# Second graph layer's low weight parts on VectorE instead of GpSimd, one behind each head's front part

## What is computed

```python
def gat_layer(x, W, att_src, att_dst, bias, src, dst, heads, out_ch, concat):
    h = (x @ W.T).reshape(n, heads, out_ch)
    a_src = jnp.einsum('nhc,hc->nh', h, att_src)
    a_dst = jnp.einsum('nhc,hc->nh', h, att_dst)
    e = jax.nn.leaky_relu(a_src[src] + a_dst[dst], NEG_SLOPE)
    m = jax.ops.segment_max(e, dst, num_segments=n)
    ex = jnp.exp(e - m[dst])
    denom = jax.ops.segment_sum(ex, dst, num_segments=n)
    alpha = ex / (denom[dst] + EPS)
    out = jax.ops.segment_sum(alpha[:, :, None] * h[src], dst, num_segments=n)
    ...
h = gat_layer(x, W1, att_src1, att_dst1, b1, src, dst, heads=8, out_ch=128, concat=True)
h = jax.nn.relu(h)
out = gat_layer(h, W2, att_src2, att_dst2, b2, src, dst, heads=1, out_ch=768, concat=True)
```

## Time and profile before

| | us |
|---|---|
| median of 3 runs | 1350.22 |
| lowest and highest of them | 1344.23, 1350.96 |
| the profiled execution's own time | 1348.07 |
| its span, first to last instruction | 1346.5 |

### The profile page before, as it was taken

One profiled execution on the slowest core, in us unless ns is written; L12 is line 12 of the kernel. 1 busy time (PEld: TensorE's weight loads), 2 busy tenths in 40 slices (PEclk: granted clock), 3 DMA queues, 4 the chain that ended last, 5 costly groups with the idle time before them and its releaser, 6 DMA issues. The chain is left out here.

```text
span 1346.5 us, 19432 instructions
## 1 busy us (share of the span) xinstructions
PE 1280.1 (95%) x7053; PEld 1099.5 (82%) x7054; DVE 911.3 (68%) x1828; ACT 582.8 (43%) x1013; POOL 127.0 (9%) x123
## 2 busy tenths in 40 slices
PE   5999999999999999999999999999999898899997
PEld 2577659969969997666999999999998778796864
DVE  4477683473473465555859999999998778836623
ACT  2011051351350343334418888888986227502110
POOL 0000010000000000003320000000002018600101
PEclk9999999999999999999999999999999998999899
DMA  9321091410410620003158999999998310007134
GB/s 340 136 94 63 9 359 55 153 71 1 153 71 1 235 95 0 1 24 141 67 209 295 356 382 389 390 386 392 389 382 281 137 28 1 1 1 293 47 105 164
DMA packets 80687, 225.46 MB, mean 167 GB/s; under 512 B 5168, under 2 KB 17008, under 8 KB 80496
## 3 DMA queue, kind: packets, MB, share of 16 engines
q1 hardware_dynamic: 72720, 187.64, 37.7%
q0 software_dynamic: 7904, 36.97, 7.6%
HBM read 197.85 MB, written 26.74 MB: 167 GB/s over the span
## 5 line engine op out<-in xcount | busy, mean ns | idle before, releaser
L2116 DVE TENSOR_TENSOR part_slot<-slot,item_hi 128x768 fp32r<-128x768 f32 x150 | 133.5, 958 | 0.2
L1557 ACT ACTIVATE item_hi<-slot 128x768 fp32r<-128x768 f32 x156 | 118.0, 833 | 23.9 <-DMA slot<-in_e0w 19.6
L2125 DVE TENSOR_TENSOR part_slot<-slot,item_hi 128x768 fp32r<-128x768 f32 x132 | 116.6, 954 | 1.7 <-ACT item_hi L1565 1.3
L1565 ACT ACTIVATE item_hi<-slot 128x768 fp32r<-128x768 f32 x132 | 99.1, 831 | 14.6 <-DMA slot<-in_e0w 14.6
L722 PE MATMUL dve_ps<-item_hi,x_hi 128*128 128x384 f32 x288 | 99.3, 345 | 0.5 <-DVE x_lo L2305 0.3
L722 PE MATMUL act_ps<-item_hi,hid_hi 128*128 128x384 f32 x288 | 98.4, 342 | 0.3 <-DVE hid_lo L2317 0.3
L724 PE MATMUL dve_ps<-item_hi,x_lo 128*128 128x384 f32 x288 | 97.2, 338 | 0.0
L723 PE MATMUL act_ps<-part_slot,hid_hi 128*128 128x384 f32 x288 | 96.8, 336 | 0.0
L724 PE MATMUL act_ps<-item_hi,hid_lo 128*128 128x384 f32 x288 | 96.1, 334 | 0.0
L723 PE MATMUL dve_ps<-part_slot,x_hi 128*128 128x384 f32 x288 | 95.6, 332 | 0.0
L1448 ACT ACTIVATE h_t<-act_ps,par 128x256 f32<-128x256 f32 x36 | 21.1, 585 | 121.5 <-PE act_ps L833 121.5
(11 more groups left out here) (407 smaller groups left out, 3268.9 us busy)
## 6 DMA issues: line engine op xcount, KB each, us to landing
slot<-in_e0w SPq DMA_DIRECT2D x48, 2304.0 KB, 10.4
slot<-in_w SPq DMA_DIRECT2D x9, 2304.0 KB, 9.4
experts<-in_e1w SPq DMA_DIRECT2D x8, 1152.0 KB, 15.3
ea_raw<-in_edge SPq DMA_DIRECT2D x8, 1024.0 KB, 5.5
slot<-in_wqkv SPq DMA_DIRECT2D x3, 2304.0 KB, 14.8
xs<-zrow POOLq DMA_DIRECT2D x2, 3072.0 KB, 15.7
item_x<-xs SPq DMA_DIRECT2D x16, 384.0 KB, 9.6
ys<-item_y POOLq DMA_DIRECT2D x16, 384.0 KB, 6.7
```

Of the source, the lines that this page charges most:

```text
L1557: go(item_hi[j][k][:, :], slot[s][:, k * D:(k + 1) * D], ACT.Copy).then_inc(up_high[j], 1)
L1565: go(item_hi[j][k][:, :], slot[s][:, k * D:(k + 1) * D], ACT.Copy).then_inc(down_high[j], 1)
L2116: vv.tensor_tensor(part_slot[s][:, ks], slot[s][:, ks], item_hi[j][k][:, :].bitcast(F32), ALU.subtract).then_inc(up_low[j], 1)
L2125: vv.tensor_tensor(part_slot[s][:, ks], slot[s][:, ks], item_hi[j][k][:, :].bitcast(F32), ALU.subtract).then_inc(down_low[j], 1)
```

## The change

The eight low parts leave GpSimd's stream. VectorE forms them instead, low part hd behind `graph_front(hd + 2)` in turn hd of its loop (in turns 6 and 7, which have no front left to make, behind `graph_out`). The arithmetic, the wait for the high part and the semaphore that is raised are the same.

```diff
+            def low_second_layer(k):
+                ks = slice(k % 4 * D, (k % 4 + 1) * D)
+                dve.wait_ge(w_high, 2 * DC * L + 3 * DC + k + 1)
+                vv.tensor_tensor(part_slot[2 + k // 4][:, ks], slot[2 + k // 4][:, ks], part_slot[k // 4][:, ks].bitcast(F32), ALU.subtract
+                                 ).then_inc(w_low, 1)
+
...
                 if hd + 2 < GH:
                     graph_front(hd + 2, row_unit(hd + 2), v0)
+                low_second_layer(hd)
             graph_out(GH - 1)
...
-            def low_of(s, block, high, done):
-                pool.wait_ge(w_high, 2 * DC * L + 3 * DC + done + 1)
-                nc.gpsimd.tensor_tensor(part_slot[s][:, block], slot[s][:, block], high.bitcast(F32), ALU.subtract).then_inc(w_low, 1)
-
...
-                for k in {2: (0,), 3: (1,), 4: (2,), 5: (3,), 6: (4,), 7: (5, 6, 7)}.get(g, ()):
-                    ks = slice(k % 4 * D, (k % 4 + 1) * D)
-                    low_of(2 + k // 4, ks, part_slot[k // 4][:, ks], k)
```

## The result

The changed kernel took 1351.38 us, median of 20 runs (1346.67 to 1357.03), against 1347.40 for the kernel before, also 20 runs (1343.21 to 1350.96). The ratio on record is 1.0041 with a 95% interval of 1.0030 to 1.0052: 0.41% slower, or 5.5 us (4.0 to 7.0). It is estimated from all the runs and is not the quotient of the medians: these lie only 3.98 us apart, and the means 5.09 us. The forecast was a loss of 5.75 us.

A forecast was written before the change was run, and what follows sets the result against it. The prediction took VectorE to bound the middle heads of the first graph layer. Five low parts at 0.87 + 0.28 us gave 5.75 us, added to 1348.07 (profile) or 1350.22 (median); middle 1355.0 us, range 1350.3 to 1360.5.

The forecast's parts named there:

- VectorE sets the pace in the middle heads: First graph layer, middle heads: VectorE busy 7.33 of 7.51 us, so work added to its stream adds to the time.
- Five on the path, three hidden: Low parts 1 to 5 delay the weights of heads 2 to 6, 4.35 us; 0, 6 and 7 fall into waits.
- 0.87 us for the operation, 0.28 for the meeting: Each low part on the path costs 0.87 us itself plus 0.28 waiting for GpSimd's second sum, 5.75 us for five.
- The prediction's bound of 0.41: Middle heads: a low part's full wait for GpSimd's second sum, 0.41 us each, would make the loss 6.4 us.
- Nobody waits for the later exponentials: Middle heads: GpSimd's third sum starts some 0.9 us late, making the last exponential later, at no cost.
- The lost race: Rival, middle heads: GpSimd's next sum goes before the waiting low part, 1.24 us more each, 11.9 in all; chance 0.08.
- The clock: Rival: longer TensorE idle time halves its clock before head 7, loss 7.5 to 8.8 us in all; chance 0.38.
- The lower of its two prices: Clock fall before head 7: 3.3 us at half clock costs 1.7 us; the higher price was 3.0.
- The time: Whole kernel: 1355.0 us, the middle of 1353.8 and 1356.0, from a loss of 5.75 us.

The follow-up runs named there:

- e1_covered: Kernel before, with low parts 0, 6 and 7 moved to VectorE and 1 to 5 left on GpSimd; 1344.87 us, ratio 0.9989 to the kernel before.
- e2_path: Kernel before, with low parts 1 to 5 moved to VectorE and 0, 6 and 7 left on GpSimd; 1349.84 us, ratio 1.0031 to the kernel before.
- e13_after_best: Changed kernel, idle time before head 1 filled in place of its `spend`, filling behind heads 1 to 5, `xres` additions behind `out_lo`; 1347.39 us, 1.0018 to kernel before.
- e3_ahead: Changed kernel, with each low part placed ahead of the front on VectorE instead of behind it; 1351.55 us, ratio 1.0039 to the kernel before.
- e4_twice: Changed kernel, with each of low parts 1 to 5 formed twice in a row on VectorE; 1363.94 us, ratio 1.0121 to the kernel before.
- e9_after_start: Changed kernel, with 32 unused matmul calls behind head 0's turns and without head 1's `spend`; 1351.27 us, ratio 1.0038 to the kernel before.

## Why the prediction was right

- **VectorE sets the pace in the middle heads.** Right: 8.67 us a head with 8.49 of it busy, at whatever clock TensorE ran.
- **Five on the path, three hidden.** Right, and shown apart by e1_covered and e2_path. The cover of low part 0 is real but hangs on TensorE coming late to head 1's turns: in e13_after_best, without that, the part delays head 1's weights by 0.86 us, of which 0.5 comes back behind them. It is also thinner than the 2.87 us that the prediction read from one execution, 1.58 in e2_path.
- **0.87 us for the operation, 0.28 for the meeting.** Right: 0.87 by e3_ahead (4.33 us for five) and 1.15 by e2_path (5.75 for five). The 0.28 holds for one phase between the two engines; in other phases it was 0.6 to 0.7. The prediction's bound of 0.41 was the bound of that phase only. What it missed is the gap of 0.46 us, which left these heads with the change: w2 to w6 grew by 4.26 us and not by 4.6.
- **Nobody waits for the later exponentials.** Right: no wait on a GpSimd sum reached VectorE, though one sum in four was held for 0.71 us.
- **The lost race.** Fell, by the 1.23 us of the five low parts and by e4_twice, which shows GpSimd and VectorE taking turns.
- **The clock.** The lower of its two prices was right, 1.6 us ahead of head 7 against 1.7, and so was that longer idle time brings it: 22 of 22 waits of 2.23 us or more were followed by slow matmuls. In the profile of the changed kernel the clock fell in heads 4 and 6, behind 2.23 us of idle time, and was hidden there as the prediction said; ahead of head 7 it held, where the slow matmuls of head 6 had left only 1.46 us of idle time. I had expected 3.1, with the clock at full in head 6, and had not seen that a fall in head 6 shortens it. That the rival stayed away in this profile is luck in part; e9_after_start has the gap of 3.12 us, and the fall.
- **The time.** 1351.38 against 1355.0 forecast, inside 1350.3 to 1360.5 but only 1.1 us above its low end (whose own sum gives 1350.4). Half of the distance is the base, 1349.25 in the forecast where 20 runs put the kernel before at 1347.40, and not at the 1350.22 of the first three. The other half is the medians' difference of 3.98 us. As a ratio the loss is 5.5 us (4.0 to 7.0) against 5.75, and 5.42 us between w1 and w6 in the profiles (5.78 without the gap), so its size was right within what the runs tell. It also came out under 0.5%, as the prediction held more likely than not.

## What to carry to other kernels

Find out which engine sets the pace in the stage that an edit touches, by a window from one turn to the next. Work moved to that engine was paid in full here, even though the engine is idle a third of the whole span and the operation takes half as long there. When moving work between GpSimd and VectorE, look at the inputs: in these traces an operation with two tensors in SBUF had to take turns with GpSimd's sums and low parts, which read SBUF too, and its price was its own time plus nearly all that was left of GpSimd's instruction. That makes place and phase part of the cost, for four columns as for 768. And check in the profile how many instructions a filling call becomes before its result is read.

## What the runs showed that I had not expected

- An operation on 4 columns took 1.19 us in place of 0.16 beside GpSimd's sums of 1.25 us. The wait came from what GpSimd was running, not from the size of the operation that waited.
- A clock at half came behind as little as 1.95 us of idle time, and in the same execution (e3_ahead) another gap of 1.95 us left the clock at full. Behind all 22 waits of 2.23 us or more it came. It costs 1.6 us where TensorE is the bound (w6 to the end, 15.4 for 13.7) and nothing where it isn't.
- Filling 4.2 of the 4.33 idle us ahead of head 1, in place of the `spend` behind them, kept the clock at 1.00 and made the kernel before 0.28% faster (0.13% to 0.43%).
